# Count build of a graph layer: another order for casts and nibbles, scaled one-hots in two-step scalar operations, closing matmuls of one column

## The reference

```python
deg  = segment_sum(ones, col); dinv = deg ** -0.5 (0 where deg is 0)
norm = dinv[row] * dinv[col]
for l in range(5):
    edge_fea = concat([edge_attr[:, 3:] @ ew1[l], edge_attr[:, 0:3] @ ew2[l]])
    msg = norm[:, None] * (h[row] + edge_fea)
    agg = segment_sum(msg, col)
    h   = relu(concat([h, agg]) @ mlp_w[l] + mlp_b[l]); batch norm; relu
```

## Time and profile before

| | |
|---|---|
| median of three executions | 1694.11 us |
| span of the profiled execution | 1693.0 us |
| PE busy, DVE busy, ACT busy over the span | 86%, 40%, 23% |
| the count build: first window's copy to last window's `ohS` (L1517 at 165.56, L1524 ends at 457.71) | 292.2 us |
| granted TensorE clock, 165.5 to 229.9 us | 0.79 of full speed |
| granted TensorE clock, 229.9 to 276.9 us | 0.94 |

### The profile page before, as it was taken

How to read it: one execution, slowest core, us unless ns; L and a number is a source line. 1 busy time by engine, 2 the same in 40 slices (tenths; PEclk the granted TensorE clock), 3 DMA queues, 4 the chain that set the end, 5 groups by cost and what they waited for, 6 DMA issues and landing times.

```text
span 1693.0 us, 24943 instructions
## 1 busy us (share of the span) xinstructions
PE 1461.4 (86%) x8538; PEld 814.1 (48%) x8539; DVE 675.2 (40%) x1560; ACT 387.6 (23%) x1010; POOL 166.6 (10%) x145
## 2 busy tenths in 40 slices
PE   3564678888889899989999899998999873999996
PEld 2553444444443444535444454534445443566664
DVE  7989777777621220122201230112201357233332
ACT  1220443434401400023001320014000330233332
POOL 1000000000000000000000000000000003466664
PEclk9875899999989999989999899999999876899999
DMA  5153000000000000000000000000004090233433
GB/s 134 38 195 108 1 1 1 1 2 1 14 2 0 14 1 0 1 15 1 0 1 0 14 1 1 1 0 13 1 0 95 7 334 20 52 63 63 66 64 40
DMA packets 49549, 57.87 MB, mean 34 GB/s; under 512 B 14319, under 2 KB 41601, under 8 KB 49184
## 3 DMA queue, kind: packets, MB, share of 16 engines
q1 hardware_dynamic: 38688, 41.67, 8.6%
q0 software_dynamic: 10752, 14.69, 5.4%
HBM read 42.36 MB, written 13.99 MB: 33 GB/s over the span
## 4 chain that ended last, share of the span: by engine, by line
PE 76%; DVE 12%; ACT 5%; issue 4%; DVEq 2%; DMA 1%; POOL 1%; SPq 0%; POOLq 0%; ACTq 0%
PE bank L654 37%; PE bank L735 13%; PE bank L1148 6%; PE bank L1163 6%; ACT at L1618 3%; PE bank L1752 3%; PE bank L1154 1%; PE bank L644 1%; DVE ohL L1409 1%; PE bank L1697 1%; PE bank L738 1%; PE bank L1750 1%; PE bank L1140 1%; DVE ohS L1524 1%; DVEq L505 1%
## 5 line engine op out<-in xcount | busy, mean ns | idle before, releaser
L654 PE MATMUL bank<-at,m 125*128 125x500 fp8e4 (+1 forms) x3500 | 698.8, 356 | 9.4 <-issue 3.1
L654 PEld LDWEIGHTS bank<-at,m 125*128 125x128 f16 x3500 | 319.0, 98 | 345.9 <-issue 39.0
L663 DVE TENSOR_TENSOR aggT<-bank,dinvB 128x500 f32<-128x500 f32 (+1 forms) x70 | 42.2, 620 | 345.8 <-PE bank L654 345.8
L826 ACT ACTIVATE hT<-bank,prm 128x500 f32<-128x500 f32 (+1 forms) x70 | 40.5, 630 | 602.8 <-PE bank L738 602.8
L874 POOL TENSOR_TENSOR idJ<-idJ,wts 125x1400 f32<-125x1400 f32 x2 | 8.0, 4005 | 1406.0 <-DVE idJ L1032 1406.0
L735 PE MATMUL bank<-hT,wcur 128*128 128x500 f32 (+1 forms) x280 | 125.3, 570 | 0.0
L788 DVE BATCH_NORM_STATS2 zst<-hT 128x6 f32<-128x500 f32 (+1 forms) x70 | 40.3, 617 | 199.9 <-ACT hT L826 199.9
L735 PE MATMUL bank<-aggT,wcur 128*128 128x500 f32 (+1 forms) x280 | 116.9, 540 | 0.0
L1148 PE MATMUL bank<-w1s,xtT 128*128 x224 | 109.3, 611 | 0.1
L1163 PE MATMUL bank<-w2s,h1T 128*128 x448 | 106.1, 380 | 1.4 <-ACT h1T L939 1.4
L623 DVE SCALAR_TENSOR_TENSOR m<-bank,dinvP,m 125x256 f16<-125x256 f32 x100 | 48.0, 483 | 148.2 <-ACT m L635 148.2
(11 more groups left out here) (319 smaller groups left out, 1446.7 us busy)
## 6 DMA issues: line engine op xcount, KB each, us to landing
slrow<-sl_dram SPq DMA_DIRECT2D x26, 512.0 KB, 4.8
w1s<-in_L_ffn_W SPq DMA_DIRECT2D x1, 4096.0 KB, 14.2
w2s<-in_L_ffn_W SPq DMA_DIRECT2D x1, 4096.0 KB, 18.9
xin<-in_x SPq DMA_DIRECT2D x1, 2800.0 KB
x<-in_x SPq DMA_DIRECT2D x1, 2800.0 KB
out_rows<-x SPq DMA_DIRECT2D x1, 2800.0 KB
xn_dram<-xn SPq DMA_DIRECT2D x1, 2800.0 KB
wraw<-in_L_gnn_mlp_w SPq DMA_DIRECT2D x5, 512.0 KB, 3.6
```

The costliest lines, as they stand in the source:

```text
L654: last = pe.matmul(bank[banks[g % len(banks)]][:, 0:w], m[:, s, k, h * 128:(h + 1) * 128], at_block(g // H)[:, s, :], start=s == 0 and k = ...
L663: dve.tensor_tensor(aggT[:, h, a:a + w], bank[banks[g % len(banks)]][:, 0:w], dinvB[:, a:a + w], ALU.mult).then_inc(s_agge, 1)
```

## The change

1. DVE does both nibble steps of pair `u` after odd window 2u + 3, one behind the other, and nothing after even windows.
2. ACT, in turn `u`, copies pair `u`, does its other work, and then casts pair `u` itself; before, it cast pair `u - 1`. For the last block of `at`, which lies where `ohS` of the even side is, the casts wait for the last pair's closing (`s_cnt`).
3. The scaled one-hot of the places is built chunk by chunk: for each of the eight chunks one operation with two steps, `is_equal` against the chunk's place and `mult` by its power of 16, both read per partition from `now` (bf16). L1520 and L1524 go, and with them one wait. `iotaS` and `ohS` lose the layout in pairs of chunks; `ohS` has the same size.
4. The closing matmuls (L1756, L1758) are one column wide.

```diff
-                    dve.wait_ge(s_now[side], (past + i) * 2 + 1)
-                    dve.tensor_tensor(ohS[side][:, :, :, :], to_all(iotaS[:, :, :], U // 2), by_pairs(now[:, side, 12, :], 128), ALU.is_equal).then_inc(s_now[side], 1)
+                    dve.wait_ge(s_now[side], past + i + 1)
                     dve.tensor_tensor(ohD[side][:, :, :, :], to_all(iotaD2[:, :, :], U // 2), by_pairs(nowKD[:, side, 1, :], W), ALU.is_equal)
                     dve.tensor_tensor(cnt1[side][:, :, :, :], to_all(iotaK[:, :, :], U // 2), by_pairs(nowKD[:, side, 0, :], GW), ALU.is_equal)
-                    dve.wait_ge(s_now[side], (past + i) * 2 + 2)
-                    dve.tensor_tensor(ohS[side][:, :, :, :], ohS[side][:, :, :, :], by_pairs(now[:, side, 13, :], 128), ALU.mult).then_inc(s_oh[side], 1)
+                    for j in range(U):
+                        last = dve.tensor_scalar(ohS[side][:, j, :], iotaS[:, :], now[:, side, 12, j:j + 1], now[:, side, 13, j:j + 1], ALU.is_equal, ALU.mult)
+                    last.then_inc(s_oh[side], 1)
...
-                if w > 1:
-                    (high_nibbles if side else low_nibbles)(w // 2 - 1)
+                if side and w > 1:
+                    low_nibbles(w // 2 - 1)
+                    high_nibbles(w // 2 - 1)
...
-            for u in range(PAIRS + 1):
-                if u < PAIRS:
-                    act.wait_ge(s_cnt, u + 1)
-                    if u >= 2:
-                        act.wait_ge(s_at, u - 1)
-                    act.activation(encI[:, u % 2, :], bank[u % 2][0:P, 0:GROUPS * PW], ACT.Copy).then_inc(s_enc, 1)
-                if u:
-                    v = u - 1
...
+            for u in range(PAIRS):
+                act.wait_ge(s_cnt, u + 1)
+                if u >= 2:
+                    act.wait_ge(s_at, u - 1)
+                act.activation(encI[:, u % 2, :], bank[u % 2][0:P, 0:GROUPS * PW], ACT.Copy).then_inc(s_enc, 1)
...
+                if q == NQ - 1:
+                    act.wait_ge(s_cnt, PAIRS)
+                for odd in range(2):
+                    act.wait_ge(s_nib, 2 * u + 1 + odd)
...
-                        last = pe.matmul(out_w, ohS[side][:, j // 2, :, j % 2], cnt1[side][:, j // 2, :, j % 2].rearrange("p (g n) -> p g n", g=GROUPS),
+                        last = pe.matmul(out_w, ohS[side][:, j, :], cnt1[side][:, j // 2, :, j % 2].rearrange("p (g n) -> p g n", g=GROUPS),
...
-                    pe.matmul(bank[u % 2][:, 0:GROUPS * PW], zeros[:, 0:128], nought(GROUPS * PW), start=False, stop=True).then_inc(s_cnt, 1)
+                    pe.matmul(bank[u % 2][:, 0:1], zeros[:, 0:128], nought(1), start=False, stop=True).then_inc(s_cnt, 1)
...
-                    pe.matmul(sums_of(b), zeros[:, 0:12], nought(sums_of(b).shape[1]), start=False, stop=True).then_inc(s_s4, 1)
+                    pe.matmul(sums_of(b)[:, 0:1], zeros[:, 0:12], nought(1), start=False, stop=True).then_inc(s_s4, 1)
```

More of the change, by code:

```diff
@@ L154, in gnn_ffn_program @@
         iotaD = r("iotaD", [128, P + 1], I16)
-        iotaS = r("iotaS", [128, 128, 2], BF16)
+        iotaS = r("iotaS", [128, 128], BF16)
         iotaD2 = r("iotaD2", [128, W, 2], I16)
@@ L165, in gnn_ffn_program @@
         encI = r("encI", [P, 2, GROUPS * PW], I32)
-        ohS_1 = r("ohS_1", [128, U // 2, 128, 2], BF16)
+        ohS_1 = r("ohS_1", [128, U, 128], BF16)
         assert r.at <= dinvB_at + 2 * 4 * N
@@ L189, in gnn_ffn_program @@
         r = Region((NT * 6 * CQ + 31) // 32 * 32)
-        ohS_0 = r("ohS_0", [128, U // 2, 128, 2], BF16)
+        ohS_0 = r("ohS_0", [128, U, 128], BF16)
         ohD_0 = r("ohD_0", [128, U // 2, W, 2], BF16)
@@ L1258, in _ @@
             pool.iota(iotaK[:, :, :], pattern=[[KEY, GROUPS], [1, W], [0, 2]], base=0, channel_multiplier=0)
-            pool.iota(iotaS[:, :, :], pattern=[[1, 128], [0, 2]], base=0, channel_multiplier=0, allow_small_or_imprecise_dtypes=True).then_inc(s_mem, 1)
+            pool.iota(iotaS[:, :], pattern=[[1, 128]], base=0, channel_multiplier=0, allow_small_or_imprecise_dtypes=True).then_inc(s_mem, 1)
             pool.memset(zt[:, :], 0.0).then_inc(s_cst, 1)
@@ L1536, in _ @@
             assert NW % 2
-            high_nibbles(PAIRS - 2)
-            low_nibbles(PAIRS - 1)
-            high_nibbles(PAIRS - 1)
+            for u in range(PAIRS - 2, PAIRS):
+                low_nibbles(u)
+                high_nibbles(u)
             attribute_sums(NQ - 2)
@@ L1628, in _ @@
                     rows_out((2 * u + 1) // SB - 1)
+                a = PW * u
+                q, n = a // CQ, min(PW, N - a)
+                a -= CQ * q
+                if q == NQ - 1:
+                    act.wait_ge(s_cnt, PAIRS)
+                for odd in range(2):
+                    act.wait_ge(s_nib, 2 * u + 1 + odd)
+                    byte = (encI[:, u % 2, :] if odd else encB[:, :]).bitcast(U8).rearrange("p (g n k) -> p k g n", g=GROUPS, k=4)
+                    for f in range((FIELDS + 1 - odd) // 2):
+                        field = odd + 2 * f
+                        last = act.activation(at_block(q)[:, field:field + FIELDS * (GROUPS - 1) + 1:FIELDS, a:a + n],
+                                              byte[:, f, :, 0:n], ACT.Copy, saturate=False,
+                                              accum_out=sums[:, FIELDS * u + field:FIELDS * u + field + 1])
+                last.then_inc(s_at, 1)
             for b in range(NQ - 2, NQ):
```

## The result

The changed kernel takes 1666.94 us (median of four executions, 1663.64 to 1672.42) against 1694.61 us of the kernel before beside it (four executions, 1692.88 to 1699.19): a ratio of 0.9843, with a 95% interval of 0.9826 to 0.9860. The forecast was 1666. The profiled execution took 1666.33 us and has a span of 1664.6.

What follows compares the result with a forecast made beforehand. No engine was full; DVE waiting for ACT's casts, in a ring of pairs, bound the build. Build 292.2 to 261.6 us gives 30.6, less 2.6 for PE and hand-over: 28 off span 1693.0, so 1665, median 1666; range 1657 to 1704.

Steps and rivals of the forecast that it cites:

- The ring: In the count build, DVE waits for ACT's casts, which wait for DVE's window: 8.8 of about 9.4 us a pair.
- the slack of 3.4: After the reorder, ACT finishes casts and copy 4.5 us after the window's end, 3.4 us before DVE's next low nibbles.
- DVE's window: One window of the build on DVE without waits: 3.44 us before, 3.54 after, with eight steps replacing two operations.
- The step: One two-pointer operation on 128 bf16 elements in DVE's window: 0.307 us long, the next starting 0.227 later.
- the f32 row's 0.274 us: Size-independent part of a 407 ns two-pointer operation on 256 elements, used to price a step.
- The main risk: Rival: DVE's queue holds too few operations, exposing the 2.42 us of loop end and loads; 1703 or 1731 us, chance 0.16.
- The evictions: Eight DVE operations in the build, 0.60 us each, 4.8 us in all.
- 2.6 us off: Taken from the build's 30.6 us gain for buffers PE still reads and the nibbles' hand-over, leaving 28 us.
- 261.6: The build's sum in us: windows, nibbles, evictions, attribute sums and last window, against 292.2 before.
- The tail: From the last one-hots to the dense units: 8.35 us, same links in another order, narrow closing worth 0.3.
- 2.42 us of queue: In DVE's window, the loop's end and three loads before the next window's first operation; claimed to hide under the steps.
- 0.84 of nibbles: DVE's nibble work for one pair in the build: 0.84 us, 30 pairs making 25.2 us.

Runs made afterwards that it cites:

- half steps: The changed kernel with each two-step operation cut in two of 64 columns, sixteen a window; 1758.44 us in one execution.

## Why the prediction was right, and where its terms were off

**The ring opens, and the order costs nothing.** Right. The wait of L1486 on the casts is gone, the kernel with the order alone shows that the order did it, and ACT's 4.1 us a pair of waiting for the nibbles bears out the slack of 3.4.

**DVE's window.** Forecast 3.54 us, measured 3.48 to 3.51. The step was forecast 0.307 long and 0.227 apart, and came out at 0.306 and 0.223; the fixed part, read from a two-pointer operation on f32, holds for the bf16 pointers. The Trainium skill, "DVE: scalar operands, raw-bit mode, write accounting and state across instructions", section 1, says that a bf16 scale costs what an fp32 one does; by that rule the f32 row's 0.274 us carries over, and the 0.28 us of the half steps agree.

**The queue.** The main risk did not come true: the loads hide, as the forecast had it. The trace of before could not settle it; the changed kernel holds nine unstarted operations and the one with half steps 11. The Trainium skill, "Advanced Engine Details and Errata", section "Engine Queue Depths", gives VectorE eight. By eight, the half steps' loop end would have come with the start of the eighth, 173.93 + 7 x 0.206 = 175.37; it came at 174.9. The measurement decides: here more than eight stand.

**The evictions** were the mis-sized term: 8 x 0.60 = 4.8 us forecast. Measured in the gaps of DVE behind the eight windows with an eviction are 12.6 us: the same eight, 6.9 us of waiting for PE's dense groups, and 0.9 of hand-over. PE's lag was seen, with 2.6 us off for buffers that PE still reads; it showed at another place, at the evictions, and cost some 5 us more than the 2.6. The shorter windows gave back 62 x 0.04 = 2.5. So the build took 266.9 us, where 261.6 + 2.6 = 264.2 were forecast.

**The tail.** Forecast 8.35 less 0.3 for the closing; measured 9.6. The closing is worth 0.2 by itself (8.2 with the closings alone), but PE's lag puts dense work ahead of the last window, 1.3 us net.

**The last stretch.** "After the build nothing is changed, so the gain stays": it stays, but the last stretch moves by itself. Build and tail together gave 24.7 us by the means of two profiles, against a forecast of 28.3 (28.0 for the build and 0.3 for the tail); the spans fell by 28.2. The 3.6 us that build and tail fell short were nearly made good outside them, in work that the change doesn't touch: that the time came within a microsecond of the forecast is to that extent luck. From the first L669 matmul to the end, in the first profiles of the kernel before and of the changed one (PE, PEld, DVE, ACT, POOL busy, clock, DMA):
```profile
500.75:1693.00 1192.25, 1105.69 (x4915) 593.65 (x4915) 302.24 (x782) 232.53 (x560) 158.55 (x116) 0.95 0.14 31
479.28:1664.60 1185.32, 1099.56 (x4915) 590.18 (x4915) 301.97 (x782) 232.53 (x560) 158.58 (x116) 0.96 0.15 31
```
DVE and ACT are busy as long as before. PE takes 6.1 us less for the same 4915 matmuls (second profiles: 1103.7 and 1100.5 us), and TensorE's granted clock is higher: between 900 and 960 us behind the first L669 matmul it is 0.68 and 0.71 of full speed in the two profiles of before, 0.76 and 0.74 in those of the changed kernel. The spread of the last stretch (1188.4 and 1192.3 in the kernel before, 1186.4 to 1192.1 in the other kernels) covers most of the gain. Why TensorE's clock differs there, and why the changed kernel's two profiles, 1185.4 and 1186.4, are the lowest of all twelve (if only just: 1186.4 with the closings alone) is not explained, and no run here was made to explain it.

**The parts.** The forecast gave one sum and no worth for each part. The runs do: the order gives the whole, 31.7 us of build (its tail takes back 2.1); the narrow closings are worth 5.3 us on the closed ring and none on the open one; the two-step operations cost 15.0 us on the closed ring and some 6 on the open one. That the loads could be hidden without the steps, and that the nibbles behind the odd window already cover one of the two gaps of a pair, stood in the prediction's own rows (2.42 us of queue, 0.84 of nibbles), and it did not draw that line.

## What to carry to other kernels

When two engines wait for each other round a ring, reorder so that the one takes what the other did a turn ago, and measure that alone before adding work to the engine that waits: here the reordering had all of the gain, and a part that came with it took some of the build's back. An operation of 128 columns with two pointers is nearly all fixed cost here (0.28 of 0.306 us), so eight of them stand against two wide ones only if they hide something; look first whether the steps of the queue can be moved ahead of an operation that waits. When an engine stops waiting, its next waits are those for its neighbours: forecast their place from the order of the other engine's work, not as a lump.

## What was not expected of the hardware

DVE's queue had handed over 11 operations that had not started. A two-pointer operation fell by only 13 ns from 306 when its columns were halved. And a stretch of some 1190 us of unchanged work differed by 3.9 us between two profiles of the same kernel, more than the 3.4 us that the medians can tell apart.
